# Layer 0's keys and values ahead of its queries, and a regrouped end, in a two-layer cross-attention and FFN kernel

## The chip, the cores and the metric

The kernel runs on one core of a Trainium2 chip. The time is the device time of one execution in microseconds (us), the median of several runs. PE is TensorE (PEld its weight loads), DVE is VectorE, ACT is ScalarE, POOL is GpSimd and SP is SyncE, which only issues DMAs. ACT issues some DMAs too.

## The reference, cut to what matters

The input is `x`, 8 tiles of 128 tokens by 512 values, and a context of the same shape. Four blocks follow each other, each added to `x` and each fed by a layer norm of it:

```python
x = x + L0_xattn(layernorm(x), ctx)   # Q = xn @ Wq + bq; K = ctx @ Wk + bk; V = ctx @ Wv + bv; 32 heads on 8 kv heads
x = x + L0_ffn(layernorm(x))          # router, 4 of 16 experts and a shared one
x = x + L1_xattn(layernorm(x), ctx)   # 32 heads of 128 on 4 kv heads
x = x + L1_ffn(layernorm(x))

def L1_ffn(xf):
    h = relu(layernorm(xf @ gw1.T + gb1) * gamma + beta)   # 32 columns a token
    gates = h @ gw2.T + gb2                                # 8 experts
    top_v, top_i = top_k(gates, 2); top_g = softmax(top_v)
    allowed = counts_of_each_expert_over_all_tokens <= capacity
    tmp = (xf @ lora_A) * w_of_each_expert                 # 128 columns a token
    return xf @ weight.T + (tmp @ lora_B) / 16
```

The count over all tokens is the one place in the last block where every tile needs every other.

## The kernel before, in words

The 8 tiles are worked in two halves of 4. Each engine's program is a hand-written list of calls; engines meet only at semaphores, and each engine runs its list strictly in order. PSUM has 8 banks, handed to PE's groups by `banks.take(n, piece, free)`, which makes PE wait until the bank's last reader is done. Products that need near-fp32 accuracy split each factor into a high and a low part (`_hi` is written by ACT, `_lo` by DVE) and use three matmuls (`three`).

**A normalization** of a tile (group `g`, tile `k`) goes: `norm_stats` on DVE (L403, L404), one `norm_sqrt` on ACT for a group of four (L411), `norm_recip` on DVE (L416), `norm_scale` on DVE (L433) into one of a few row buffers, `norm_turn` on PE (four 128x128 transposes, L442), `norm_hi` on ACT (L450 in groups 0 and 1, L453 elsewhere) and, from group 2 on, `norm_lo` on DVE (L460). Group 7 is the second half's rows for the last block. `mm_group` (L466) is the matmul line of nearly all products.

**The opening of layer 0.** `sync_attention0` issues the first loads on SP's queue in the order of the code. PE transposes `consts` 32 times (`WARM`, L698), turns the 4 normalized tiles of half 0 and computes queries 0 and 1 of half 0, the keys, queries 2 and 3, and the values of 4 tiles. A query (`query(half, m)`) and the keys are products of 512 columns in plain fp32, written out by ACT (`q0T_hi`, L758; `k0T_hi`, L750) and DVE (`q0T_lo`, L877; `k0T_lo`, L865), then sent by ACT's queue to DRAM (`q_rows`, L500; `k_rows`, L495). SP reads them back in another layout (`q0st`, L553 and L555; `k0bd`, L537 and L539). ACT splits the output weights (`wo_hi`, L763) in between. Next PE turns half 1's tiles, computes its keys and its query 0, and only then starts the scores (L645) of tile 0, which need all four queries of half 0 from DRAM. DVE has two jobs beside: the row maxima (`mx`, L886) of the scores and the normalization of half 1.

**The end.** Layer 1's attention runs 32 steps a half. In step `i` of the second half, `ending(i)` adds work of the last block: group 6's normalization, the adapter weights' split, and from `i == STEPS` the first half's small products. `tensor_small(h, 0)` is the gate product `h` of half `h` (32 columns), `tensor_small(h, 1)` the LoRA product `tmp` (128 columns) followed by the turn of `hT` (L2232). Then `tensor_adapters`: the dense products of tiles 0 to 3, with the turns of group 7 between them, both small products of half 1, the dense products of tiles 4 to 6 (`dense_open`, L2323, left open in their banks), the counts matmul (L2340), the dense product of tile 7, the turns of the expert weights `we` (L2347) and the LoRA products (L2358). DVE's gate work of half `h` is `vector_gating(h, 0..4)`: the norm of `h` (L2274 to L2289), the product with `gw2` (L2291 to L2294), the top two (L1298 to L2298), and the weights from the softmax (L2302 to L2306). ACT gives it a square root (j = 0, L2259) and an exponential (j = 3, L2262). `dense_add` (L2381) adds a dense product to `x`; L2413 adds the LoRA part, after which SP stores the tile.

```python
        def ending(i, weights, norm, norm_next, small):
            if STEPS - 4 <= i < STEPS:
                norm(6, i - STEPS + 7)
            if i == STEPS - 1:
                norm_next(7, 0)
            if i >= STEPS:
                small(0, i - STEPS)
```

Of the kernel before, what the change touches and what calls it, by code (L numbers as in the profile page):

```python
# [14 lines left out]
P = 128  # L15
# [109 lines left out]
def three(hi_lo_a, hi_lo_b):  # L125
    (ah, al), (bh, bl) = hi_lo_a, hi_lo_b
    return (ah, bh), (ah, bl), (al, bh)
# [38 lines left out]
def layers_kernel(nc, A, out):  # L166
    with ExitStack() as whole:
# [304 lines left out]
        WARM = 32  # L472
# [34 lines left out]
        def sync_attention0():  # L507
            load = nc.sync.dma_start
            load(consts[:, :], A["consts"]).then_inc(S["ld_consts"], 16)
            for b in range(HB):  # L510
                load(x[:, b, :], A["x"][b]).then_inc(S[f"rows_in{b}"], 16)
            load(wq[:, :, :], A["wq0"]).then_inc(S["ld_wq0"], 16)
            load(wkv[:, 0], A["wkv0"][:, 0]).then_inc(S["ld_wk0"], 16)
            load(ctxT[0][:, :, :], A["ctxT"][0]).then_inc(S["ld_ctx00"], 16)
            load(bq[:, :], A["bq0"]).then_inc(S["ld_bqk0"], 16)
            load(bk[:, :], A["bk0"]).then_inc(S["ld_bqk0"], 16)
            load(wkv[:, 1], A["wkv0"][:, 1]).then_inc(S["ld_wv0"], 16)
            load(bv[:, :], A["bv0"].broadcast_to([P, P])).then_inc(S["ld_wv0"], 16)
# [93 lines left out]
        def tensor_attention0():  # L612
# [133 lines left out]
        def scalar_attention0():  # L746
# [47 lines left out]
            norm_sqrt(0)  # L794
            for k in range(HB):
                norm_hi(0, k)
            query(0, 0)
            act.wait_ge(S["q0_lo"], 1)
            queries_out(nc.scalar, 0, 0)
            query(0, 1)  # L800
            act.wait_ge(S["q0_lo"], 2)
            queries_out(nc.scalar, 0, 1)
            keys(0)
            act.wait_ge(S["k0_lo"], 1)
            keys_out(nc.scalar, 0)
            norm_sqrt(1)
# [55 lines left out]
        def vector_attention0():  # L862
# [52 lines left out]
            query(0, 0)  # L915
            dve.wait_ge(S["ld_x_rest"], 16 * HB)
            norm_stats(1, 0)
            norm_stats(1, 1)
            query(0, 1)
            norm_stats(1, 2)  # L920
            keys(0)
            norm_stats(1, 3)
            query(0, 2)
            norm_recip(1)
            norm_scale(1, 0)
            query(0, 3)
            for k in range(1, HB):
                norm_scale(1, k)
            for b in range(HB):
                values(b)  # L930
# [1279 lines left out]
        def scalar_ending(i):  # L2210
            ending(i, scalar_adapter_weights, scalar_norm, scalar_norm, scalar_small)

        def vector_ending(i):
            ending(i, vector_adapter_weights, vector_norm, vector_norm, vector_small)

        def tensor_small(h, j):
            if j == 0:
# [7 lines left out]
            ps = banks.take(next(out_banks), ("tmp", h), (S["tmpT"], h + 1))  # L2225
            mm_group(ps[:, :], [q for k in range(KT) for q in three(
                (ws[0][:, k, 0:P], ws[1][:, k, 0:P]),
                (xn1[h][0][:, k, :], xn1[h][1][:, k, :]))]).then_inc(S["tmp_mm"], 1)
            ps = banks.take(next(out_banks), ("h_t", h), (S["gate_sc"], h + 3))
            pe.wait_ge(S["scT"], h + 3)  # L2230
            for b in range(HB):
                ins = nc.tensor.transpose(ps[:, b * G1:(b + 1) * G1], hT[h][:, b * P:(b + 1) * P],  # L2232
                                          ident[0:G1, 0:G1])
            ins.then_inc(S["gate_t"], 1)
# [83 lines left out]
        def tensor_adapters():  # L2318
# [6 lines left out]
            for b in range(HB):  # L2325
# [16 lines left out]
            dense_open(B - 1)  # L2342
            for h in range(2):
# [5 lines left out]
                ins.then_inc(S["we_t"], 1)  # L2349
            for b in range(B):  # L2350
# [10 lines left out]
        def scalar_adapters():  # L2361
            for b in range(HB):
                scalar_norm(7, b + 1)
            for j in (5, 6):
                scalar_norm(7, j)
            for j in (0, 3):
                scalar_gating(0, j)
            for j in range(2):
                scalar_small(1, j)
            for j in (0, 3):  # L2370
                scalar_gating(1, j)
# [4 lines left out]
        def vector_adapters():  # L2376
            for b in range(HB):
                vector_norm(7, b + 1)
# [3 lines left out]
            for j in (5, 6):  # L2382
                vector_norm(7, j)
            for j in range(5):
                vector_gating(0, j)
            for j in range(2):
                vector_small(1, j)
            for j in range(5):
                vector_gating(1, j)
# [152 lines left out]
```

## Time and profile before

| | before |
|---|---|
| median of 3 runs | 1236.09 us |
| lowest and highest run | 1232.84 and 1236.33 us |
| the profiled execution's time | 1236.35 us |
| its span, first to last instruction | 1235.0 us |
| PE busy | 1185.1 us, 96% |
| DVE busy | 805.3 us, 65% |
| ACT busy | 671.4 us, 54% |
| POOL busy | 419.6 us, 34% |
| mean granted TensorE clock | 0.992 |

The profiled execution takes 1.35 us more than its span. The chain that ended last is 82% PE, 7% DVE, 5% DMA and 3% ACT. A full clock (1.00) is TensorE's 2.4 GHz level, 0.50 its 1.2 GHz level. The change touches the first 50 us and the last 65.

### The profile page before, as it was taken

Reading aid. Unit: us, or ns where it says so; the run is one execution under the profiler, and the core shown is the slowest. Engines: PE = TensorE matmul, PEld = TensorE weight load, DVE = VectorE, ACT = ScalarE, POOL = GpSimd, SP = SyncE. Lnnn points to the kernel's source line nnn. Section 1 sums busy time; section 2 is a strip of 40 time slices with the busy share of each in tenths; the row PEclk is TensorE's granted clock in tenths of the full one; section 3 lists DMA queues with packets and bytes.
Section 4 is the critical chain, followed back from the end, with each engine's and each line's share of the span. In section 5 each row is a group of like instructions: output and inputs, shape, how many; then the busy total and the mean of one; then the engine's idle time right before and its main releaser. Section 6 shows DMA issues by size and latency. Waiting matters only on the chain.

```text
span 1235.0 us, 16580 instructions
## 1 busy us (share of the span) xinstructions
PE 1185.1 (96%) x5948; PEld 913.7 (74%) x5948; DVE 805.3 (65%) x1511; ACT 671.4 (54%) x1562; POOL 419.6 (34%) x515
## 2 busy tenths in 40 slices
PE   8989999899999999799999999999999999999997
PEld 5646556577776777688888888877888888888765
DVE  3457777677766784756666567764566666677757
ACT  2245741577777883355555555643455555556621
POOL 2413434577777761022223232310122232322200
PEclk9999999999999999899999999999999999999999
DMA  8675422885788777221112122211221121221101
GB/s 290 173 172 133 155 77 102 300 205 103 153 212 248 155 143 190 71 57 60 60 44 68 43 62 67 61 52 53 70 63 46 44 68 60 61 68 27 59 1 68
DMA packets 72849, 127.93 MB, mean 104 GB/s; under 512 B 11640, under 2 KB 30968, under 8 KB 70072
## 3 DMA queue, kind: packets, MB, share of 16 engines
q1 hardware_dynamic: 53024, 73.90, 20.1%
q0 software_dynamic: 17296, 48.26, 15.7%
q10 hardware_dynamic: 2448, 4.72, 1.1%
q8 instruction: 47, 0.77, 0.3%
q14 instruction: 34, 0.28, 0.1%
HBM read 150.37 MB, written 26.48 MB: 143 GB/s over the span
## 4 chain that ended last, share of the span: by engine, by line
PE 82%; DVE 7%; DMA 5%; ACT 3%; issue 2%; SPq 0%; ACTq 0%; POOL 0%; POOLq 0%; DVEq 0%
PE bank L466 50%; PE bank L1220 11%; PE bank L2008 7%; PE bank L1984 4%; PE bank L679 2%; PE bank L693 2%; PE bank L1280 2%; PE bank L645 1%; PE bank L660 1%; PE bank L1241 1%; DMA wf_raw<-in_wffn,weight_row 1%; DMA q0st<-m0T 1%; DMA lb_raw<-in_lb 1%; DMA returned<-moe 1%; DMA q_rows<-q0T_lo 1%
## 5 line engine op out<-in xcount | busy, mean ns | idle before, releaser
L1976 POOL TENSOR_SCALAR p<-p,mx 128x256 f32<-128x256 f32 x256 | 162.8, 652 | 524.4 <-DVE mx L1970 524.4
L1187 DVE TENSOR_TENSOR wf_lo<-wf_raw,wf_hi 128x512 fp32r<-128x512 f32 x188 | 121.5, 688 | 33.8 <-ACT wf_hi L1181 29.1
L1962 ACT ACTIVATE p<-bank,mx 128x256 f32<-128x256 f32 x256 | 118.0, 485 | 10.7 <-DVE mx L1952 10.5
L466 PE MATMUL bank<-xnA_hi,w1q_hi 128*128 128x512 f32 x288 | 118.6, 412 | 3.6 <-DVE xnA_lo L460 3.2
L1181 ACT ACTIVATE wf_hi<-wf_raw 128x512 fp32r<-128x512 f32 x192 | 110.1, 625 | 9.4 <-DMA wf_raw<-in_wffn,weight_row 9.0
L466 PE MATMUL bank<-xnA_hi,w1q_lo 128*128 128x512 f32 x288 | 114.6, 398 | 0.0
L466 PE MATMUL bank<-xnA_lo,w1q_hi 128*128 128x512 f32 x288 | 114.1, 396 | 0.0
L1991 ACT ACTIVATE p1T_hi<-bank 128x512 fp32r<-128x512 f32 x128 | 75.1, 596 | 65.7 <-PE bank L1984 65.7
L1916 ACT ACTIVATE q1T_hi<-bank 128x512 fp32r<-128x512 f32 x64 | 38.2, 597 | 132.2 <-PE bank L466 132.2
L466 PE MATMUL bank<-w1o_hi,a1T_hi 128*128 128x512 f32 x256 | 105.2, 411 | 0.1
L466 PE MATMUL bank<-wf_raw,zT 128*128 128x512 f32 x220 | 102.9, 593 | 2.2 <-DVE x L1263 1.3
L1922 DVE TENSOR_TENSOR q1T_lo<-bank,q1T_hi 128x512 fp32r<-128x512 f32 x64 | 44.2, 691 | 93.0 <-ACT q1T_hi L1916 93.0
L466 PE MATMUL bank<-w1o_hi,a1T_lo 128*128 128x512 f32 x256 | 100.3, 392 | 0.0
L466 PE MATMUL bank<-w1o_lo,a1T_hi 128*128 128x512 f32 x256 | 100.2, 391 | 0.0
L1603 POOL DMA_INDIRECT moe<-ys,token_out x47 | 82.1, 1746 | 28.1 <-issue 12.5
L2041 DVE TENSOR_TENSOR x<-bank,x 128x512 f32<-128x512 f32 x64 | 44.2, 690 | 71.8 <-PE bank L466 71.6
L1996 DVE TENSOR_TENSOR p1T_lo<-bank,p1T_hi 128x512 fp32r<-128x512 f32 x128 | 86.2, 681 | 0.0
L1948 DVE TENSOR_REDUCE mx<-bank 128x2 f32<-128x512 f32 x128 | 81.5, 677 | 0.0
L1220 PE MATMUL bank<-wf_hi,xsT_hi 128*128 128x512 f32 x188 | 78.4, 417 | 1.1 <-DVE xsT_lo L1293 1.1
L1984 PE MATMUL bank<-consts,p 128*128 128x128 f32 x512 | 75.5, 273 | 2.1 <-DVE a1T_lo L2019 2.1
L1220 PE MATMUL bank<-wf_lo,xsT_hi 128*128 128x512 f32 x188 | 74.1, 394 | 0.0
L1582 POOL DMA_INDIRECT wf_raw<-in_wffn,weight_row x47 | 50.5, 1075 | 66.9 <-PE bank L466 29.1
(338 smaller groups left out, 2958.8 us busy)
## 6 DMA issues: line engine op xcount, KB each, us to landing
w_raw<-in_wq SPq DMA_DIRECT2D x64, 256.0 KB
w_raw<-in_wo SPq DMA_DIRECT2D x64, 256.0 KB
moe<-xn SPq DMA_DIRECT2D x2, 2304.0 KB, 11.7
returned<-moe SPq DMA_DIRECT2D x8, 512.0 KB, 7.8
q0st<-q_rows SPq DMA_DIRECT2D x14, 256.0 KB, 4.6
x<-in_x SPq DMA_DIRECT2D x8, 256.0 KB, 6.5
ctx<-in_ctxT SPq DMA_DIRECT2D x2, 1024.0 KB, 10.8
q_rows<-q0T_hi ACTq DMA_DIRECT2D x8, 256.0 KB
```

What stands on the lines that cost most here:

```text
L466: ins = nc.tensor.matmul(ps, a, b, start=(n == 0), stop=(n == len(pairs) - 1))
L1181: nc.scalar.activation(wf[m % 2][0][:, a, c, :], raw[m % STREAMS][:, a, c, :], ACT.Copy).then_inc(S["gu_hi"], 1)
L1187: nc.vector.tensor_tensor(wf[m % 2][1][:, a, c, :], raw[m % STREAMS][:, a, c, :], wf[m % 2][0][:, a, c, :].bitcast(F32), ALU.subtract).the ...
L1220: ins = nc.tensor.matmul(ps[:, :], a, c, start=(k == 0 and t == 0), stop=(k == KT - 1 and t == 2))
L1603: nc.gpsimd.indirect_dma_start(out=moe[j % 2], out_offset=bass.IndirectOffsetOnAxis(ap=token_out[:, at:at + 1], axis=0), in_=ys[j % Y_RING ...
L1948: ins = nc.vector.tensor_reduce(m[:, 2 * n:2 * n + 2], banks.of(("s1", s, n))[:, :].rearrange("p (h k) -> p h k", h=2), AX.X, ALU.max)
L1962: ins = nc.scalar.activation(pr1[s % 2][:, h, :], banks.of(("s1", s, n))[:, hh * 2 * P:(hh + 1) * 2 * P], ACT.Exp, bias=m[:, UH + h:UH + h ...
L1976: ins = nc.gpsimd.tensor_scalar(pr1[s % 2][:, h, :], pr1[s % 2][:, h, :], m[:, 3 * UH + h:3 * UH + h + 1], 1.0, ALU.mult, ALU.mult)
L1984: ins = nc.tensor.transpose(ps[:, h * P:(h + 1) * P], pr1[s % 2][:, h, part * P:(part + 1) * P], ident)
L1991: nc.scalar.activation(p1T[0][:, part, :], banks.of(("t1", s, part))[:, :], ACT.Copy).then_inc(S["p1T_hi"], 1)
L1996: nc.vector.tensor_tensor(p1T[1][:, part, :], banks.of(("t1", s, part))[:, :], p1T[0][:, part, :].bitcast(F32), ALU.subtract).then_inc(S[" ...
L2008: ins = nc.tensor.matmul(ps[:, :], a, c, start=(part == 0 and n == 0), stop=(part == 1 and n == 2))
```

## The change

In the opening, the loads are issued in another order: the key weights and the context ahead of `x`, the query weights last. PE computes keys and values of half 0 ahead of the queries, with the turns between the values, and `WARM` is 20. ACT and DVE follow. At the end, DVE takes the statistics of group 7 tile by tile in steps STEPS-1 to STEPS+1, ACT the square root of group 7 in step STEPS+1, with a first square root of a constant in step STEPS-1. PE takes the gate product of half 1 between the dense products of tiles 1 and 2, and its turn ahead of the LoRA product. DVE's gate work of both halves is interleaved with the dense additions. The dense product of tile 7 goes behind the turns of `we`. No arithmetic is added but ACT's square root of one column.

```diff
-        WARM = 32
+        WARM = 20
...
             load(consts[:, :], A["consts"]).then_inc(S["ld_consts"], 16)
+            load(wkv[:, 0], A["wkv0"][:, 0]).then_inc(S["ld_wk0"], 16)
+            load(ctxT[0][:, :, :], A["ctxT"][0]).then_inc(S["ld_ctx00"], 16)
             for b in range(HB):
                 load(x[:, b, :], A["x"][b]).then_inc(S[f"rows_in{b}"], 16)
+            load(wkv[:, 1], A["wkv0"][:, 1]).then_inc(S["ld_wv0"], 16)
+            load(bk[:, :], A["bk0"]).then_inc(S["ld_bqk0"], 16)
+            load(bq[:, :], A["bq0"]).then_inc(S["ld_bqk0"], 16)
+            load(bv[:, :], A["bv0"].broadcast_to([P, P])).then_inc(S["ld_wv0"], 16)
             load(wq[:, :, :], A["wq0"]).then_inc(S["ld_wq0"], 16)
...
-            for k in range(HB):
+            keys(0, 7)
+            values(0, 4)
+            values(1, 5)
+            for k in range(2):
                 norm_turn(0, k, k)
-            query(0, 0, 4)
-            query(0, 1, 5)
-            keys(0, 7)
-            query(0, 2, 0)
-            query(0, 3, 1)
-            for b, n in enumerate((2, 3, 4, 5)):
-                values(b, n)
+            values(2, 6)
+            for k in range(2, HB):
+                norm_turn(0, k, k)
+            values(3, 4)
+            for m, n in enumerate((5, 6, 0, 1)):
+                query(0, m, n)
...
         def scalar_ending(i):
-            ending(i, scalar_adapter_weights, scalar_norm, scalar_norm, scalar_small)
+            if i == STEPS - 1:
+                nc.scalar.activation(hr[:, 0:1], eps, ACT.Sqrt)
+            if i == STEPS + 1:
+                norm_sqrt(7)
+            ending(i, scalar_adapter_weights, scalar_norm, nothing, scalar_small)
 
         def vector_ending(i):
-            ending(i, vector_adapter_weights, vector_norm, vector_norm, vector_small)
+            ending(i, vector_adapter_weights, vector_norm, vector_norm, nothing)
+            for k in (2, 3):
+                if i == STEPS + k - 2:
+                    dve.wait_ge(*norm_x_ready(7, k))
+                    norm_stats(7, k)
...
-            for b in range(HB):
-                if b >= 2:
-                    norm_turn(7, b - 2, next(out_banks))
...
-            for k in range(2, HB):
-                norm_turn(7, k, next(out_banks))
-            for j in range(2):
-                tensor_small(1, j)
-            for b in range(HB, B - 1):
+            for b in range(2):
+                for k in (2 * b, 2 * b + 1):
+                    norm_turn(7, k, next(turn_banks))
+                dense(b)
+            tensor_small(1, 0)
+            dense(2)
+            tensor_small(1, 2)
+            tensor_small(1, 1)
+            dense(3)
+            for b in range(HB, B - 2):
                 dense_open(b)
...
-            dense_open(B - 1)
+            dense_open(B - 2)
...
+            dense_open(B - 1)
             for b in range(B):
...
         def scalar_adapters():
...
+            norm_hi(7, 0)
+            norm_hi(7, 1)
+            scalar_gating(0, 0)
+            norm_hi(7, 2)
+            norm_hi(7, 3)
+            scalar_small(1, 0)
+            scalar_gating(1, 0)
+            scalar_gating(0, 3)
+            scalar_small(1, 1)
+            scalar_gating(1, 3)
...
         def vector_adapters():
...
+            norm_recip(7)
+            norm_scale(7, 0)
+            norm_scale(7, 1)
+            vector_small(0, 1)
+            norm_scale(7, 2)
+            norm_lo(7, 0)
+            norm_lo(7, 1)
+            norm_scale(7, 3)
+            vector_gating(0, 0)
+            vector_gating(0, 1)
+            norm_lo(7, 2)
+            norm_lo(7, 3)
+            dense_add(0)
+            vector_gating(0, 2)
+            vector_gating(0, 3)
+            dense_add(1)
+            vector_small(1, 1)
+            vector_gating(1, 0)
+            dense_add(2)
+            vector_gating(1, 1)
+            vector_gating(0, 4)
+            vector_gating(1, 2)
+            vector_gating(1, 3)
+            dense_add(3)
+            vector_gating(1, 4)
```

In the opening DVE's list becomes: scales of tiles 0 and 1 each followed by a tile's values, scales of tiles 2 and 3, keys, values 2 and 3, query 0, statistics of half 1's first two tiles, query 1, the other two, query 2, reciprocal and scale of half 1's tile 0, query 3, the other scales. ACT's is: square root, keys high, `norm_hi` four times, keys out, then each query high and out, with half 1's square root behind query 1 and two `wo_hi` behind queries 2 and 3 each, as before.

Three places show the order that results. First SP's queue in the opening, before and after; `wkv` is loaded twice, the keys' part first:

```order
L509 DMA consts<-in_consts 128x149
L511 DMA x<-in_x 128x512 x4
L512 DMA wq_66<-in_wq 128x2048
L513 DMA wkv_68<-in_wkv 128x512
L514 DMA ctx_0_64<-in_ctxT 128x2048
L515 DMA bq_86<-in_bq 128x4
L516 DMA bk_87<-in_bk 128x1
L517 DMA wkv_68<-in_wkv 128x512
L518 DMA bv_88<-in_bv 128x128
```

```order
L509 DMA consts<-in_consts 128x149
L510 DMA wkv_68<-in_wkv 128x512
L511 DMA ctx_0_64<-in_ctxT 128x2048
L513 DMA x<-in_x 128x512 x4
L514 DMA wkv_68<-in_wkv 128x512
L515 DMA bk_87<-in_bk 128x1
L516 DMA bq_86<-in_bq 128x4
L517 DMA bv_88<-in_bv 128x128
L518 DMA wq_66<-in_wq 128x2048
```

The query weights went from second to last, the keys' weights and the context to the front. Second, PE in the opening; `xn_58`, `xn_59`, `num` and `den` are the four normalized tiles, and the 128x128 products are values:

```order
-L698 MATMUL bank<-consts 128x128 x32
+L698 MATMUL bank<-consts 128x128 x20
+L466 MATMUL bank<-ctx_0_64,wkv_68 128x512 x4
+L466 MATMUL bank<-wkv_68,ctx_0_64 128x128 x8
 L442 MATMUL bank<-consts,xn_58 128x128 x4
 L442 MATMUL bank<-consts,xn_59 128x128 x4
+L466 MATMUL bank<-wkv_68,ctx_0_64 128x128 x4
 L442 MATMUL bank<-consts,num 128x128 x4
 L442 MATMUL bank<-consts,den 128x128 x4
```

Keys and two tiles of values now stand ahead of the turns; the values no longer stand between the last query and the turns of half 1. Third, ACT from step STEPS-1 on, before and after; `xnA` is half 0's normalized input, `xnB` half 1's:

```order
L2015 ACTIVATE a1T_hi<-bank 128x512
L453 ACTIVATE xnA_hi<-bank 128x4x128
L1991 ACTIVATE p1T_hi<-bank 128x512 x2
L2015 ACTIVATE a1T_hi<-bank 128x512
L2240 ACTIVATE hT_242<-bank,gb_240 32x512
L2244 ACTIVATE tmpT_259<-bank 128x512
L411 ACT_TABLE_LOAD
L411 ACTIVATE rstd<-moments,consts 128x4
```

```order
L2015 ACTIVATE a1T_hi<-bank 128x512
L2212 ACT_TABLE_LOAD
L2212 ACTIVATE hr<-consts 128x1
L453 ACTIVATE xnA_hi<-bank 128x4x128
L1991 ACTIVATE p1T_hi<-bank 128x512 x2
L2015 ACTIVATE a1T_hi<-bank 128x512
L2250 ACTIVATE hT_242<-bank,gb_240 32x512
L411 ACTIVATE rstd<-moments,consts 128x4
L2254 ACTIVATE tmpT_259<-bank 128x512
```

The table load and one short square root moved ahead of the last tile of `xnA_hi` and the last `p1T_hi`, and group 7's square root ahead of `tmpT`.

## Rows read from the trace of the kernel before

**Rows 1.** Chain of waits, opening: start us, length us, what worked or was waited for
```profile
2.59 5.21 DMA x<-in_x
...
12.72 14.02 PE bank L466 x32
...
32.69 6.71 DMA q_rows<-q0T_lo
```
**Rows 2.** Timeline, opening: start, length, engine, line, operation, count, [idle before <- releaser]
```profile
30.00 3.73 PE L466 MATMUL bank<-wkv,ctx 128*128 128x128 f32 x32
...
31.28 0.75 DVE L877 SCALAR_TENSOR_TENSOR q0T_lo<-bank,bq,q0T_hi 128x512 fp32r<-128x512 f32 x1 [2.38 <-ACT q0T_hi L758]
...
42.81 0.94 PE L645 MATMUL bank<-k0bd,q0st 96*128 96x256 f32 x6 [0.23 <-DMA q0st<-q_rows]
```
**Rows 3.** Timeline, SP's issues in the opening: start, length of the issue
```profile
4.01 0.43 SPq L514 DMA_DIRECT2D ctx<-in_ctxT  x1
...
6.59 0.68 SPq L518 DMA_DIRECT2D bv<-in_bv  x1
```
**Rows 4.** DMA issues, opening: KB each, us from issue to landing
```profile
ctx<-in_ctxT SPq DMA_DIRECT2D x1, 1024.0 KB, 10.2
bv<-in_bv SPq DMA_DIRECT2D x1, 64.0 KB, 10.4
```
**Rows 5.** DMA queues, 26 to 27 us (q10 is ACT's): packets, MB, share
```profile
q10 hardware_dynamic: 106, 0.20, 52.8%
```
**Rows 6.** Stretches: PE, PEld, DVE, ACT, POOL busy us (count), PEclk, DMA share, GB/s
```profile
42.80:47.30 4.50, 3.13 (x15) 2.12 (x16) 3.97 (x7) 0.51 (x1) 3.99 (x4) 1.00 0.96 212
47.30:50.70 3.40, 3.40 (x17) 3.40 (x18) 1.85 (x4) 0.00 (x0) 0.00 (x0) 0.51 0.71 190
...
1201.10:1204.20 3.10, 3.10 (x9) 1.28 (x8) 2.56 (x12) 1.58 (x2) 0.00 (x0) 0.50 0.02 5
```
**Rows 7.** Chain of waits, end
```profile
1191.16 2.80 PE bank L466 x12
1193.96 0.44 PE bank L442 x4
...
1199.81 0.69 DVE xnB_lo L460
...
1209.60 0.30 DVE h__244 L2251
...
1218.87 0.38 DVE chosen L2390
```
**Rows 8.** Timeline, end
```profile
1173.63 1.25 DVE L1996 TENSOR_TENSOR p1T_lo<-bank,p1T_hi 128x512 fp32r<-128x512 f32 x2
...
1174.81 0.39 PE L2008 MATMUL bank<-p1T_hi,v_hi 128*128 128x512 f32 x1
...
1181.87 0.69 DVE L2041 TENSOR_TENSOR x<-bank,x 128x512 f32<-128x512 f32 x1 [4.18 <-PE bank L466]
...
1219.38 0.37 PE L2340 MATMUL bank<-chosen,ones 128*128 128x16 f32 x2 [1.49 <-DVE chosen L2390]
...
1222.43 1.03 PE L2347 MATMUL bank<-consts,we 128*128 128x128 f32 x8
...
1227.05 1.28 DVE L2413 TENSOR_TENSOR x<-bank,x 128x512 f32<-128x512 f32 x2
```
**Rows 9.** Groups of DVE, 1184 to 1235 us: busy us, mean ns | idle before
```profile
L460 DVE TENSOR_TENSOR xnB_lo<-bank,xnB_hi 128x512 fp32r<-128x512 f32 x4 | 2.8, 692 | 0.8 <-ACT xnB_hi L453 0.8
L2381 DVE TENSOR_TENSOR x<-bank,x 128x512 f32<-128x512 f32 x4 | 2.8, 691 | 5.5 <-PE bank L466 5.5
...
L433 DVE TENSOR_SCALAR xn<-x,moments,rstd 128x512 f32<-128x512 f32 x4 | 2.2, 538 | 0.0
```
**Rows 10.** Timeline, a table load and what follows it on ACT at 51 us
```profile
51.47 1.28 ACT L827 ACT_TABLE_LOAD   x1
...
52.76 0.20 ACT L827 ACTIVATE preload<-consts 128x1 f32<-128x1 f32 x1
```

More of the change, by code:

```diff
@@ L794, in scalar_attention0 @@
             norm_sqrt(0)
+            keys(0)
             for k in range(HB):
                 norm_hi(0, k)
[L797 to L803, printed above, removed]
             act.wait_ge(S["k0_lo"], 1)
             keys_out(nc.scalar, 0)
+            for m in range(2):
+                query(0, m)
+                act.wait_ge(S["q0_lo"], m + 1)
+                queries_out(nc.scalar, 0, m)
             norm_sqrt(1)
@@ L914, in vector_attention0 @@
                 norm_scale(0, k)
-            query(0, 0)
-            dve.wait_ge(S["ld_x_rest"], 16 * HB)
[L917 to L926, printed above, removed]
+                if k < 2:
+                    values(k)
+            keys(0)
+            values(2)
+            values(3)
+            dve.wait_ge(S["ld_x_rest"], 16 * HB)
+            for m in range(KT):
+                query(0, m)
+                if m < 2:
+                    norm_stats(1, 2 * m)
+                    norm_stats(1, 2 * m + 1)
+                if m == 2:
+                    norm_recip(1)
+                    norm_scale(1, 0)
             for k in range(1, HB):
                 norm_scale(1, k)
-            for b in range(HB):
-                values(b)
             keys(1)
@@ L2224, in tensor_small @@
                 return
[L2225 to L2234, printed above, removed]
+            if j == 1:
+                ps = banks.take(next(out_banks), ("tmp", h), (S["tmpT"], h + 1))
+                mm_group(ps[:, :], [q for k in range(KT) for q in three(
+                    (ws[0][:, k, 0:P], ws[1][:, k, 0:P]),
+                    (xn1[h][0][:, k, :], xn1[h][1][:, k, :]))]).then_inc(S["tmp_mm"], 1)
+            if j == 2 or h == 0:
+                ps = banks.take(next(out_banks), ("h_t", h), (S["gate_sc"], h + 3))
+                pe.wait_ge(S["scT"], h + 3)
+                for b in range(HB):
+                    ins = nc.tensor.transpose(ps[:, b * G1:(b + 1) * G1], hT[h][:, b * P:(b + 1) * P],
+                                              ident[0:G1, 0:G1])
+                ins.then_inc(S["gate_t"], 1)
         def scalar_small(h, j):
@@ L2323, in dense_open, with dense @@
                     nc.tensor.matmul(ps[:, :], a, c, start=(n == 0), stop=False)
-            for b in range(HB):
-                if b >= 2:
-                    norm_turn(7, b - 2, next(out_banks))
+            def dense(b):
                 ps = banks.take(next(score_banks), ("dense", b), (S["dense_add"], b + 1))
@@ L2361, in scalar_adapters @@
         def scalar_adapters():
[L2362 to L2371, printed above, removed]
+            name, value = norm_dest_free[7]
+            act.wait_ge(S[name], value)
+            norm_hi(7, 0)
[8 more added lines that the diff above has]
+            scalar_gating(1, 3)
             for h in range(2):
@@ L2376, in vector_adapters, with dense_add @@
         def vector_adapters():
-            for b in range(HB):
-                vector_norm(7, b + 1)
+            def dense_add(b):
                 dve.wait_ge(S["dense_mm"], b + 1)
```

14 lines of the change are left out of this document (removed).

## The prediction, made before the changed kernel ran

> **What bounds the kernel now.** Read the chain of waits first, for who sets the end, then the timeline of the same stretch, for how long each piece takes and what idles. The page says PE is 96% busy and 82% of the chain, so a gain needs a stretch where PE idles or works beside the chain. There are two.
>
> In the opening the chain waits for `x` to land until 7.80, runs the normalization, and from 12.72 PE works without a gap: queries 0 and 1, keys, queries 2 and 3 [rows 1]. These five products end at 30.00, 17.28 / 5 = 3.46 us each; the values follow with 3.6 [rows 2]. Then come turns, keys and query 0 of half 1 until 42.58, and the scores begin at 42.81 after 0.23 us of waiting for a load [rows 2]. That load closes a round trip: the last query's low part is ready at 32.03 [rows 2], its store lands at 39.40 [rows 1], and SP reads it back. So PE and the round trip arrive within 0.23 us of each other.
>
> At the end the chain leaves PE at 1199.81 for DVE and stays there until `chosen` at 1219.24 [rows 7]: the gate work of half 0, then of half 1, one behind the other. PE waits 1.49 us for it before the counts at 1219.38 [rows 8], and its clock is at the 0.50 level (1.2 GHz) from 1201.10 to 1204.20 [rows 6]. The counts are followed by 15.6 us to the end of the span.
>
> **The end, worked out.** The same DVE work must fit between group 7's reciprocal and the counts, but interleaved, so I add up.
>
> First a cost. ACT gets a table load and a short square root, 1.28 + 0.20 = 1.5 us [rows 10], ahead of the last `xnA_hi` and the last `p1T_hi`. Queued behind them on ACT are these; for them waits DVE (`xnA_lo`, two tiles' statistics, `p1T_lo`), and for that PE's last attention product. Now the first `p1T_lo` ends near 1174.26 and PE takes it at 1174.81 [rows 8]: 0.55 us of slack, so PE starts 1.5 - 0.55 = 1.0 us late. Bounds: 0 if the load hides, 1.5 if the slack is gone.
>
> After the switch, the trace shows the next operation at 52.76, 0.01 us behind the load's end [rows 10]. The Trainium skill (ScalarE: Activation LUTs, "What ACT_TABLE_LOAD costs") counts a drain of about 1.38 us beside the load, 2.66 in all; by that the wait would be 2.4 instead of 1.0 and the time 1.4 higher. The trace does not agree at this place, so I leave it out of the sum and keep it as a rival.
>
> DVE: its last addition of layer 1 starts at 1181.87 now [rows 8], 1182.9 then. Addition 0.69, statistics 0.87, square root and reciprocal 0.5: scales begin about 1185.0. From there: 4 scales 2.2, 4 low parts 2.8, 4 dense additions 2.8 [rows 9], two copies 0.6 (0.30 each), `chosen` 0.4 [rows 7]. A half's gate work is 1219.24 - 1209.60 = 9.64 with copy and `chosen` [rows 7], so 8.9 without; some 0.3 us a half of that is waiting for ACT, which the interleaved additions now cover. Two halves 17.3. Sum 26.1: `chosen` ends at about 1211.1.
>
> PE: its last output product ends about 1182.7. Up to the counts it has the LoRA product of half 0, four dense products, both small products of half 1 and two open dense products, 9 x 2.80 = 25.2, and four turns of `xn` and two of `hT`, 6 x 0.44 = 2.6 [rows 7]: 1210.5, and 0.4 of waiting for DVE's last low part before the gate product. So 1210.9. The two meet within 0.2 us; the counts run at about 1211.2 instead of 1219.38, **8.2 us earlier**. PE no longer idles long enough there for the fall of rows 6 to return.
>
> Behind the counts nothing shortens: one dense product, then the turns of `we` 3.05 us after the counts, first final addition 4.62 us after those turns' start [rows 8]. The other dense product (2.80) now stands between the turns and the LoRA product, where PE was idle: turns end 1215.3, dense 1218.1, first LoRA product 1218.8, against 1218.9 for DVE's first addition. It is hidden with 0.1 to spare; uncovered it costs at most 2.8. Bounds of the gain: 9.2 (no delay from the table load) and 5.4 (that product uncovered).
>
> **The opening, worked out.** What matters is T, the start of the first query on PE: 12.72 now.
>
> Landings: `x` with 1.1 MB ahead and included lands at 7.80 [rows 1], the context with 3.4 MB at 4.01 + 10.2 = 14.2 and `bv` with 3.7 MB at 6.59 + 10.4 = 17.0 [rows 3, 4]. The first two give 2.8 us per MB. In the new order the context (1.4 MB) lands at 8.6, `x` (2.4) at 11.4, `bv` (2.7) at 12.3, or at 14.3 if it keeps its lag of 2.0 behind that line; the query weights, last with 3.7 MB, between 15.0 and 17.0. I take 14 for `bv`, since the same tiny loads stand ahead of it.
>
> The keys run from 8.6 to 12.1 in front. PE then waits for `bv`, which `values` demands together with its weights. Queued behind that wait are the turns; behind `values` on DVE stands the scale of tile 1. From `bv`, PE does four values (3.6) and four turns (1.8) before the first query: T = 19.4 at `bv` 14.0, 17.7 at 12.3. I take 19. Shorter warm-up: PE idles before the keys. The clock fell at 47.3 after PE had been busy 3.13 of 4.50 us [rows 6], so it may fall here; keys at the 1.2 GHz level would take 6.9 us, until 15.5, and add about 1.5 to T at most. Dropping 12 warm-up transposes costs nothing else, since PE would wait for the context anyway.
>
> From T: four queries end at T + 13.8. Before, the values (3.6) covered the latency from the last query to half 1's normalized tiles; now the turns are next. The last query's low part ends 2.0 us behind the product (30.00 to 32.03 [rows 2]), the scales of tiles 1 to 3 follow at 0.54 each, the last turn 0.44: T + 17.9 instead of T + 15.6. A new wait of 2.3. Keys and query of half 1, 7.0: scores at T + 24.9. With T = 19 that is 43.9, against 42.81: **1.1 us later**. Break-even is T = 17.9.
>
> The round trip: 12.8 us from the last query's end to the scores would give T + 26.6 = 45.6, 2.8 later. But ACT's queue now carries five pairs of stores back to back at 0.20 MB/us [rows 5], 0.52 MB a pair, 2.6 us each; with the queries 3.46 apart and the keys' pair out of the way, the last pair has no queue ahead. I count 2 us less or more, T + 24.6, and keep 2.8 as the bound. The other bound is T = 17, a gain of 0.9.
>
> SP's queue is moved past nothing else; the number of DMAs is unchanged. POOL waits for the normalized tiles and for `wo_hi`, both later by some 4 us, beside PE's work. Everything between 50 and 1170 us I let slide with the scores: 0.
>
> **Sum.** 1235.0 - 8.2 + 1.1 = 1227.9 of span, and 1.35 around it as in the profiled execution (1236.35 against a median of 1236.09): 1229.2. The shown runs spread over 3.5 us, so I add 1.5 on both sides.
>
> **Rivals.**
> 1. *Forecast*: 1229.2. For it: both sums at the end agree. Chance 0.54.
> 2. *The opening gains.* `bv` lands on the line and the queries start at 17: -0.9 instead of +1.1, and the table load hides: 1226.2. For it: the lag of `bv` may come from what was issued with it, not from the tiny loads ahead. Chance 0.16.
> 3. *The opening pays double.* The round trip sets the scores (+2.8), or the clock falls once there and costs 1.7 (half of the 3.4 us at the lower level [rows 6]): +2.8 to +4.5, 1231 to 1232.6. Chance 0.14.
> 4. *A new wait in the end takes the cover.* DVE and PE are within 0.2 us in three places; if the dense product of tile 7 or an ACT operation queued behind another holds the chain, the gain is 5.4 instead of 8.2: 1232.0; with the delays of both, up to 1234. Chance 0.10.
> 5. *The drain of the table switch is paid*: 1230.6 by the working above. Against it: rows 10. Chance 0.03.
> 6. *Slower than before.* SP's queue serves the loads it holds together rather than in turn; then the query weights, now last of the urgent ones, land with the 3.3 MB queued behind them, 9.2 us later, T about 26.2. Opening +8.3: 1236.4, no change; with the clock at its lower level for two stretches more, 1240. It decides from T = 26.1 on, and means slower by 0.3% only from T = 29.8. Against it: `x` landed 6.4 us ahead of the context. No change 0.02, slower 0.01.
>
> That the change doesn't do what it says: the order shows that it does.
>
> **How the numbers follow.** A measurement can tell about 0.3%, 3.7 us, from no change. Faster means below 1232.4. Rival 4 and the worst of rival 3 reach over it: half of 4 and a quarter of 3, with the rest of 6, make 0.11 for no change, 0.01 for slower, 0.88 for faster. The range goes from 1224.7 (rival 2 less 1.5) to 1233.5 (rival 4's 1232.0 and 1.5 more; it holds rival 3 and 5 as well).
>
> **What would show it.** First query on PE at 19 (17.7 to 20), scores at 43.9; PE idle between the last query of half 0 and the turns of half 1. At the end: a table load at about 1171 in the old time, PE waiting about 1 us before its last attention product, no stretch at 0.50 after 1180, the counts about 28.5 us after the last output product's end instead of 37.7, and 15.6 us from counts to end. Wrong would be: counts less than 6 us earlier relative to the last output product, a first query past 22, or a difference of over 2 us grown between 50 and 1170 us.

## The result, and the profile after

The kernel before took 1235.8 us (median of 13 runs, 1232.84 to 1238.54), the changed one 1228.97 us (13 runs, 1225.48 to 1232.93). The ratio is 0.9948, with a 95% interval of 0.9935 to 0.996: 6.4 us less, between 4.9 and 8.0. The forecast was 1229.2, with a range of 1224.7 to 1233.5. The profiled execution took 1227.31 us, its span is 1226.0 (before 1236.35 and 1235.0).

The end first. The chain of waits of the changed kernel, start and length in us:

```profile
1170.36 1.28 ACT L2212
...
1174.68 0.58 DVE p1T_lo L1996
...
1175.31 1.67 PE bank L2008 x6
...
1205.15 5.48 PE bank L2333 x24
1210.64 0.13 PE bank L2354 x2
1210.76 2.83 PE bank L2333 x12
1213.59 0.45 PE bank L2361 x4
...
```

The long run of DVE in [rows 7] is gone: the chain now goes over PE's dense product (L2333), the counts (L2354), the dense product of tile 6, and the turns of `we` (L2361). A shorter run of DVE stays in the chain, from 1186.86 to 1193.14, but PE is busy beside nearly all of it. The timeline of the same stretch:

```profile
1171.66 0.20 ACT L2212 ACTIVATE hr<-consts 128x1 f32<-128x1 f32 x1
...
1175.31 0.50 PE L2008 MATMUL bank<-p1T_hi,v_hi 128*128 128x512 f32 x1 [0.76 <-DVE p1T_lo L1996]
...
1182.53 0.69 DVE L2041 TENSOR_TENSOR x<-bank,x 128x512 f32<-128x512 f32 x1 [3.37 <-PE bank L466]
...
1209.87 0.37 DVE L2424 TENSOR_REDUCE chosen<-goh 128x16 f32<-128x128 f32 x1
...
1210.47 0.29 PE L2354 MATMUL bank<-chosen,ones 128*128 128x16 f32 x2
...
1213.43 1.03 PE L2361 MATMUL bank<-consts,we 128*128 128x128 f32 x8
...
1218.06 1.28 DVE L2447 TENSOR_TENSOR x<-bank,x 128x512 f32<-128x512 f32 x2
```

PE waits 0.76 us for the last `p1T_lo`, because the table load and its square root stand ahead of it on ACT. Layer 1's last addition starts at 1182.53, against 1181.87 in [rows 8]. The counts start at 1210.47 without a wait: 27.9 us after that addition, where it was 37.5 (1219.38 less 1181.87). `chosen` ends at 1210.24, 0.2 us ahead of them. From the counts to the end of the span it is 15.5 us, as before. By stretches (us, then PE, PEld, DVE, ACT and POOL busy with counts, granted clock, DMA share, GB/s):

```profile
1183.00:1193.30 10.30, 10.09 (x55) 7.97 (x54) 8.89 (x30) 3.37 (x7) 0.00 (x0) 1.00 0.00 0
1193.30:1210.60 17.30, 17.30 (x78) 12.92 (x79) 15.25 (x66) 3.21 (x6) 0.00 (x0) 1.00 0.01 1
```

PE is busy for all but 0.2 us of 27.6, and the clock stays at 1.00; the 3.1 us at 0.50 of [rows 6] don't return.

Now the opening, timeline of PE:

```profile
2.65 4.20 PE L698 MATMUL bank<-consts 128*128 128x128 f32 x20 [2.65 <-DMA consts<-in_consts]
7.46 3.67 PE L466 MATMUL bank<-ctx,wkv 128*128 128x512 f32 x8 [0.62 <-DMA ctx<-in_ctxT]
12.77 2.05 PE L466 MATMUL bank<-wkv,ctx 128*128 128x128 f32 x16 [1.64 <-DMA bv<-in_bv]
...
18.25 13.97 PE L466 MATMUL bank<-xnF,wq 128*128 128x512 f32 x32
32.06 0.60 PE L442 MATMUL bank<-consts,xn 128*128 128x128 f32 x4
35.13 0.66 PE L442 MATMUL bank<-consts,xn 128*128 128x128 f32 x4 [2.47 <-DVE xn L433]
...
36.60 3.60 PE L466 MATMUL bank<-ctx,wkv 128*128 128x512 f32 x8
...
44.49 0.94 PE L645 MATMUL bank<-k0bd,q0st 96*128 96x256 f32 x6 [0.86 <-DMA q0st<-q_rows]
```

and the round trip of the last query in the chain of waits:

```profile
31.59 1.15 ACT wo_hi L765 x2
32.74 0.58 ACT q0T_hi L760
33.35 0.76 DVE q0T_lo L877
34.13 0.59 ACTq L500
34.76 6.48 DMA q_rows<-q0T_lo
```

The context lands about 1.2 us ahead of the forecast, `bv` 1.3 us, and the first query starts at 18.25 instead of 19. The wait ahead of half 1's turns is there (2.47). PE would be ready for the scores at about 43.6, and then waits 0.86 us for a load that closes the round trip of the last query: its product ends at 32.06 and the scores start at 44.49, 12.4 us later. They are 1.7 us later than in [rows 2]. The store takes 6.48 us, nearly as long as before (6.71, [rows 1]), and a queue stands ahead of it. The ten stores of half 0's keys and queries are 1360 packets on q10, ACT's queue, so 136 each. When the first store of the last pair was issued, the queue had moved this much, first in the kernel before (0 to 32.06 us), then in the changed one (0 to 34.13 us):

```profile
q10 hardware_dynamic: 879, 1.70, 13.7%
```

```profile
q10 hardware_dynamic: 953, 1.85, 16.2%
```

The four older pairs are 1088 packets, so 209 of them were still to go before and 135, one whole store, in the changed kernel. The queue ahead got shorter by half a store and did not vanish.

### The profile page after: what moved, and what is told of

The parts are those of the page before. It is cut to its first block, busy times and chain, and to the rows that moved or that the text cites. A ratio compares the mean times of both kernels' runs of the same rounds, so it can differ in the third digit from the quotient of the medians.

```text
span 1226.0 us, 16554 instructions
## 1 busy us (share of the span) xinstructions
PE 1180.0 (96%) x5936; PEld 911.9 (74%) x5936; DVE 804.8 (66%) x1511; ACT 669.7 (55%) x1561; POOL 419.6 (34%) x515
## 4 chain that ended last, share of the span: by engine, by line
PE 70%; POOL 7%; DVE 7%; issue 7%; DMA 5%; ACT 3%; SPq 1%; ACTq 0%; POOLq 0%; DVEq 0%
PE bank L466 46%; PE bank L2008 7%; PE bank L1220 5%; PE bank L1984 4%; POOL moe L1603 4%; POOL xs L1592 2%; PE bank L679 2%; PE bank L693 2%; DMA moe<-ys,token_out 1%; PE bank L645 1%; POOL wf_raw L1582 1%; PE bank L660 1%; DMA xs<-xn_rows,token_in 1%; PE bank L2333 1%; DMA q0st<-m0T 1%
## 5 line engine op out<-in xcount | busy, mean ns | idle before, releaser
L1948 DVE TENSOR_REDUCE mx<-bank 128x2 f32<-128x512 f32 x128 | 81.5, 677 | 0.0
```

The costliest lines, as they stand in the source:

```text
L1948: ins = nc.vector.tensor_reduce(m[:, 2 * n:2 * n + 2], banks.of(("s1", s, n))[:, :].rearrange("p (h k) -> p h k", h=2), AX.X, ALU.max)
```

## The experiments

Each ratio is against the kernel before, run on the same chip beside it. Where places are compared, they come from one profiled execution each. From the scores' start to the last row maximum of layer 1's attention (L1948) the executions of the thirteen kernels differ by up to 4.6 us (1114.0 to 1118.6), with the same code there; so a whole span tells little, and the places are compared by distances inside a stretch.

### The end alone, and the opening alone

`e1_end_only` has the changed functions of the end and the opening of the kernel before; `e2_open_only` the reverse.

> The opening as before, the end as changed. Theory A (the end gives all of it, the opening costs what its scores are late, 1.7 us at 44 us): the scores start at 42.8 and the whole is 1 to 2 us below the changed kernel, near 1227.5. Theory B (a late opening is taken up by later waits before layer 1): scores at 42.8, but the whole within 0.7 us of the changed kernel, near 1229. From the last output product of layer 1 to the end of the span both expect 43.5 us, as in the changed kernel, against 53 before.

> The opening as changed, the end as before. Theory A: scores at 44.5 and 1 to 2 us slower than before, 1237 to 1238. Theory B: scores at 44.5, but the same time as before within 0.7 us; the lateness of 1.7 us at 44 us should then be found smaller at each later landmark (138, 185, 227 us).

The end alone: 1225.72 us, ratio 0.993 (0.9916 to 0.9944), so 8.6 us less (6.9 to 10.4). The opening alone: 1236.36 us, ratio 1.0015 (1.0004 to 1.0027), so 1.9 us more (0.5 to 3.3). Together they give -6.7, the whole change measured -6.4. Both fit theory A, the end alone with a little more than the 1 to 2 us forecast. In the opening alone the scores start at 45.02, in the end alone at 42.39; from layer 1's last addition to the end it is 43.5 us with the new end and 53.2 with the old one. The old opening has its scores at 42.4 to 43.0 in its three profiled kernels, so one execution tells such a place to about half a microsecond. So the whole gain is made at the end, and the opening gives some of it back.

In the opening alone it was not the round trip that held the scores. Timeline and stretch of `e2_open_only`:

```profile
36.85 5.30 PE L466 MATMUL bank<-ctx,wkv 128*128 128x512 f32 x8
41.98 3.60 PE L466 MATMUL bank<-xnF,wq 128*128 128x512 f32 x8
45.02 1.15 PE L645 MATMUL bank<-k0bd,q0st 96*128 96x256 f32 x5
```

```profile
37.00:40.00 3.00, 3.00 (x5) 1.18 (x4) 0.00 (x0) 1.76 (x4) 3.00 (x5) 0.50 0.75 225
```

The keys of half 1 take 5.3 us instead of 3.6 at a granted clock of 0.50 (1.2 GHz), right behind the 2.47 us in which PE waited for the normalized tile. Of the seven profiled kernels that have this order of PE (the changed one, and e2, e3, e5, e6, e7, e11), five show the low clock there; of the six that have the values behind the last query (before, and e1, e4, e8, e9, e10) none does. Where PE at its low clock sets the scores, they start 12.6 to 12.7 us after the last query's end; where the round trip does (the changed kernel, e3), 12.4 to 12.5. The two nearly coincide. (`e6` is left out here: another wait holds its scores.) Why the clock fell in five and not in the changed kernel and e3, which have the same wait, stays open.

### Values back behind the last query

The load order, the keys in front and the changed end stay. DVE's list follows; its part of the edit is left out here.

```
-            values(0, 4)
-            values(1, 5)
-            for k in range(2):
-                norm_turn(0, k, k)
-            values(2, 6)
-            for k in range(2, HB):
+            for k in range(HB):
                 norm_turn(0, k, k)
-            values(3, 4)
-            for m, n in enumerate((5, 6, 0, 1)):
+            for m, n in enumerate((4, 5, 0, 1)):
                 query(0, m, n)
+            for b, n in enumerate((2, 3, 6, 4)):
+                values(b, n)
```

> The changed kernel with the values moved back behind the last query of half 0, keys and load order as changed. Theory A: the first query no longer waits for bv but for the query weights at about 16.0, against 18.25; the values cover the wait in front of half 1's turns again (2.5 us of idle PE in the changed kernel, under 0.3 here), so the scores start at 42.2 (both by PE's work and by the round trip of 12.4 us from the last query), 2.3 us earlier than changed. The whole gains 1 to 2 us if A, under 0.7 if B. Rival: the query weights land later once nothing waits between, first query at 18, scores at 44.

1226.34 us, ratio 0.9932 (0.9918 to 0.9946). Timeline of PE:

```profile
15.48 13.97 PE L466 MATMUL bank<-xnF,wq 128*128 128x512 f32 x32 [1.16 <-DMA wq<-in_wq]
29.29 3.73 PE L466 MATMUL bank<-wkv,ctx 128*128 128x128 f32 x32
32.86 1.27 PE L442 MATMUL bank<-consts,xn 128*128 128x128 f32 x8
...
42.78 0.95 PE L645 MATMUL bank<-k0bd,q0st 96*128 96x256 f32 x6 [0.91 <-DMA q0st<-q_rows]
```

The queries no longer wait behind `bv`, and the values again cover the latency to half 1's turns. The scores are back at 42.8. With 13.5 us from the last query's end to the scores it is the round trip that holds them; PE is ready 0.9 us earlier. I had counted on 12.4 us and 42.2. The last pair found 231 older packets ahead of it in ACT's queue (857 of 1088 moved by 31.36), against 135 in the changed kernel, so queries that end 2.8 us earlier gave only 1.7. The order of the values is what the opening loses by, not the order of the loads: the trace shows it, and the medians agree (2.0 us), though the intervals of the two ratios overlap.

### The table load one step later

```
-            if i == STEPS - 1:
+            if i == STEPS:
                 nc.scalar.activation(hr[:, 0:1], eps, ACT.Sqrt)
```

> The changed kernel with ACT's constant square root, and so its table load, one step later (behind the last a1T_hi instead of ahead of the last xnA_hi). Theory A: PE's wait of 0.76 us before its last attention product goes, all that follows moves up by 0.8 us relative to the last step, and the table load still hides, since ACT idles there for over 2 us. Rival: the load then delays hT of half 0 and with it the LoRA bank, and nothing is gained. In the whole 0.8 us is near the limit of what the comparison tells; the trace decides.

1228.17 us, ratio 0.9944 (0.9929 to 0.9958). Timeline:

```profile
1174.74 0.39 PE L2008 MATMUL bank<-p1T_hi,v_hi 128*128 128x512 f32 x1
...
1176.92 1.28 ACT L2212 ACT_TABLE_LOAD   x1
```

PE's wait is gone. From the last row maximum of layer 1 (L1948) to the last output addition it takes 21.2 us here and 22.3 in the changed kernel; the kernel before has 21.2. All profiled kernels with the load at its early place have 22.3 or 22.4, all with it later or without it 21.2 or 21.3. So the load costs 1.1 us where the change put it and nothing one step later. In the medians this is too small to be seen (0.9944 against 0.9948).

### The dense product of tile 7 back ahead of the turns

```
             dense_open(B - 2)
+            dense_open(B - 1)
             for h in range(2):
...
-            dense_open(B - 1)
             for b in range(B):
```

> The changed kernel with the dense product of tile 7 back ahead of the turns of we; nothing else differs. The prediction's working: between turns and the first LoRA product PE has nothing but this product, so with it ahead the turns start one dense product (2.8 us) later, at 1216.4 on the changed kernel's clock, and the last six additions follow: end of span 2.3 to 2.8 us later, from the last output addition to the end 46 instead of 43.5, 1231 to 1232. Rival (DVE or ACT, still at work on we, holds the turns anyway, so that the product was hidden in either place): less than 0.5 us.

1230.86 us, ratio 0.9971 (0.9956 to 0.9987), 2.8 us more than the changed kernel's ratio gives, though the intervals touch; the trace decides. Chain of waits, and the timeline of PE behind the turns:

```profile
1213.07 0.14 PE bank L2354 x2
1213.21 5.58 PE bank L2333 x24
1218.79 0.45 PE bank L2362 x4
```

```profile
1218.63 1.03 PE L2362 MATMUL bank<-consts,we 128*128 128x128 f32 x8
1221.45 0.47 PE L2373 MATMUL bank<-lb_hi,la_hi 128*128 128x512 f32 x1 [1.78 <-issue]
```

Now 5.58 us of dense products stand between counts and turns instead of 2.83, and PE idles 1.78 us behind the turns. From the last output addition to the end it is 46.3 us against 43.5. The product costs its full 2.8 ahead of the turns and nothing behind them, where DVE and ACT work on `tw` and `la`.

### What makes the last store slow

SP reads nothing of the queries back before all four stores of half 0 have landed.

```
         for m in range(KT):
+            sp.wait_ge(S[f"st_q{m}"], 32)
+        for m in range(KT):
```

> The changed kernel, where SP starts no read of the queries' rows before all four stores of half 0 have landed. It tells what makes the last query's store land 6.5 us after it was issued. Theory A (SP's reads share the path with ACT's stores): the last store lands 3 to 4.5 us after its issue, and ACT's queue moves about 0.20 MB in each us of its flight; the scores may still be later, since four reads now follow one another. Theory B (stores of ACT's own queue, issued before, stand ahead of it): it lands 6 to 7 us after issue as before, with the queue still at 0.1 to 0.2 MB/us, and the scores are 2 to 4 us later.

One execution, 1234.43 us. Chain of waits:

```profile
36.61 4.62 DMA q_rows<-q0T_lo
...
50.23 1.78 DMA q0st<-q_rows
```

The last store lands 4.62 us after its issue, against 6.48. The queues (q1 is SP's, q10 ACT's; packets, MB, share), 34 to 35 us in the changed kernel:

```profile
q1 hardware_dynamic: 88, 0.04, 14.2%
q10 hardware_dynamic: 63, 0.12, 44.1%
```

and alone, 28 to 29 us and 34 to 35 us in this kernel:

```profile
q10 hardware_dynamic: 105, 0.20, 53.1%
```

```profile
q10 hardware_dynamic: 46, 0.09, 39.5%
```

The two microseconds of this kernel have no reads beside them, and one moves less than the changed kernel with reads. While the last store flies the queue moves 0.05 to 0.19 MB in each us, not the 0.20 of theory A, and the kernel before moved 0.20 to 0.21 from 28 to 30 us with SP's reads beside it. So the reads are not what sets the rate here. What theory B names is there too: when the last store was issued, 315 packets were left to move, itself included (1045 of 1360 moved by 36.61), in the changed kernel 369 (991 by 34.76), in the kernel before 427 (933 by 32.69). The times to landing go the same way: 4.62, 6.48 and 6.71 us. That is 68, 57 and 64 packets in a us. At the changed kernel's 57 the smaller queue alone would give 5.5 us, so about half of the 1.9 us is the queue ahead; the rest, at most 0.9 us, may be the reads or the spread of the rate, and one execution does not part them.

Holding the reads back is no way out: SP then issues them one behind the other, 0.43 us each, and the scores start at 52.15. I had expected 2 to 4 us for that; it was 7.7, of which 1.9 because its queries ended later. Of those 1.9 us, 0.2 are a later `bv` and 1.7 the clock: behind its wait of 1.95 us for `bv` the granted clock was 0.50 from 15 to 17 us, over the values and the turns, where the changed kernel has 1.00.

### The biases' load, the warm-up

`e11_bv_first` issues `bv` ahead of `x`; `e7_warm32` has 32 warm-up transposes again.

> The changed kernel with one load moved: bv goes out ahead of x instead of behind the value weights and the small biases. PE waits for bv 1.6 us ahead of the values in the changed kernel. If bv's own landing is what holds the first query: that wait goes or falls to about 0.3 (the value weights land next), the first query starts at 17 instead of 18.3, the scores at 43 instead of 44.5, ratio 0.994. If the value weights issued with it land as late, or x lands later because of the broadcast load ahead of it: first query at 18 to 19 and no change, 0.9948.

> The changed kernel with the old number of warm-up transposes, 32 instead of 20. The prediction's step: PE waits for the context and then for bv anyway, so the twelve cost nothing either way. Keys would start when the transposes end, about 2.5 us later than 7.5, at 9.3 to 10, or at the context's landing; the values would still start at bv, 12.8, and the first query at 18.3. Rival (keys then end after bv has landed): the first query 0.2 to 1 us later. The clock stays at its high level in both.

With `bv` first: 1227.54 us, ratio 0.9945 (0.9925 to 0.9964), no change. PE then waits for the value weights instead, 0.98 us, and the values start at 12.53 instead of 12.77. It was not `bv` alone that was late but what was issued with it. With the warm-up (one execution, 1230.68 us) the keys start at 7.62 instead of 7.46, the values at 12.94 and the first query at 18.42. The warm-up makes no difference that can be told here; my 9.3 to 10 for the keys was wrong, because the twelve added transposes take only 0.9 us (5.11 against 4.20). The clock stayed high up to the queries but fell at the keys of half 1, which I had not expected.

### Towards a better version

`e8_best` joins the values behind, the late table load and the changed end. `e9_end_late_table` is the opening of the kernel before with the changed end and the late table load. `e10_wq_first` is `e8_best` with the query weights loaded ahead of the value weights:

```
-            load(wkv[:, 1], A["wkv0"][:, 1]).then_inc(S["ld_wv0"], 16)
             load(bk[:, :], A["bk0"]).then_inc(S["ld_bqk0"], 16)
             load(bq[:, :], A["bq0"]).then_inc(S["ld_bqk0"], 16)
-            load(bv[:, :], A["bv0"].broadcast_to([P, P])).then_inc(S["ld_wv0"], 16)
             load(wq[:, :, :], A["wq0"]).then_inc(S["ld_wq0"], 16)
+            load(wkv[:, 1], A["wkv0"][:, 1]).then_inc(S["ld_wv0"], 16)
+            load(bv[:, :], A["bv0"].broadcast_to([P, P])).then_inc(S["ld_wv0"], 16)
```

> The changed kernel with two of its pieces corrected: the values of half 0 stand behind the last query again (the keys stay in front, the loads keep the new order), and the constant's square root that brings ACT's table stands one step later. Theory A (the two measured apart add up: values behind gave 2.6 us over the changed kernel, the later table 0.7): 1225 to 1226 beside a kernel before of 1235.8, ratio 0.992 to 0.993; first query on PE near 15.5, scores near 42.8, no wait of PE ahead of its last attention product, 43.5 us from layer 1's last output addition to the end. Theory B (the later table gives nothing, since the same wait of PE turns up at another operation): the ratio of the kernel with the values behind alone, 0.9932.

> The opening of the kernel before, the changed end, and the table's load one step later. If the new opening with the values behind is worth nothing over the old opening, this runs level with the combination of all three (within 0.1%), 1225 to 1226, ratio 0.992 to 0.993; if the keys in front still gain, it is slower than that by 0.5 to 1 us. Against the same kernel without the later table (ratio 0.993) it should gain 0.5 to 1.0 us; scores at 42.4, PE without a wait ahead of its last attention product.

> The kernel with values behind, late table and changed end, and now the query weights loaded right behind x, ahead of the value weights and bv, since the first query waited for them 1.2 to 1.7 us. Theory A (the scores follow the end of the last query by a round trip of 12.4 to 13.7 us, so what brings the first query forward brings the scores forward): first query at 15.0 to 15.3 instead of 16.0, scores at 41.8 to 42.2, about 0.7 us less than that kernel, ratio 0.992 to 0.993. Theory B (the loads share the path, so that the order of the last three changes nothing): first query at 15.5 to 16.0, ratio as before, 0.9935.

| kernel | median us | ratio (95%) | last query's product ends | scores start |
|---|---|---|---|---|
| changed | 1228.97 | 0.9948 (0.9935 to 0.996) | 32.06 | 44.5 |
| e8_best | 1225.42 | 0.9937 (0.9916 to 0.9958) | 29.83 | 42.7 |
| e9_end_late_table | 1226.1 | 0.9927 (0.9905 to 0.9949) | 29.2 | 43.0 |
| e10_wq_first | 1225.09 | 0.9912 (0.9896 to 0.9928) | 29.14 | 42.5 |

`e8_best`, `e9_end_late_table` and the two kernels e1 and e4 can't be told apart (0.9927 to 0.9937). So the later table load did not show in the medians beside e1 or e4, and keys in front with the values behind gained nothing over the old opening. The three kernels with the changed end that have the changed order of PE in the opening and tile 7's product where the change put it (the changed one, e3, e11) lie at 0.9944 to 0.9948. `e10_wq_first` has the lowest ratio of all, 10.9 us less than before (8.9 to 12.8), and its interval lies below the changed kernel's: by these five runs it beats both, though it was not run beside the changed kernel. Its interval overlaps those of `e8_best`, `e9_end_late_table`, e1 and e4. Its first query starts at 15.30 and waits only for the turned tiles, so the loads bound it no longer. But the scores gained 0.1 us against `e8_best`, not 0.7, since the round trip took 13.4 us instead of 12.9:

```profile
31.83 6.98 DMA q_rows<-q0T_lo
```

The places explain 0.1 us of the difference between these two; the rest of the 0.25% is inside the intervals and is not shown. The last query's product ends anywhere from 29.1 to 30.0 in the six kernels with the values behind, and SP's first read behind the last store is issued at 38.7 to 39.7 without a relation to it (29.14 and 38.83 in e10, 29.2 and 39.73 in e9, 29.83 and 38.86 in e8). In all six ACT's queue still holds older stores when the last pair comes (181 packets in e8, where it comes at 31.90, 209 in the kernel before at 32.06, 248 in e10 at 31.21, 280 in e1 at 31.13), so an earlier last query finds a longer queue ahead, and gains little.

## Why the prediction was right, step by step

The forecast time of 1229.2 us came within 0.3 us of the median. That is closer than the steps deserve: a difference of 7.1 us was forecast and 6.4 measured, the end gave 0.4 more than worked out and the opening cost 0.8 more, and the mechanism in the opening was not the one forecast.

**The end, -8.2 forecast.** The sum was right in mechanism and 0.4 us low: alone it measured -8.6, and from layer 1's last addition to the end 9.7 us went (53.2 to 43.5), where I had 9.2 before taking off the 1.0 of the table load. `chosen` took 27.7 us from that addition where the sum gave 28.2. PE's and DVE's ends meet within 0.2 us, as worked out, and neither waits for the other for long.

**The table load, 1.0.** Right: 1.1 us by the late placing. The operation behind the load starts 0.02 us after its end (1170.36 and 1.28, then 1171.66). Rival 5 with its drain of 1.38 us falls. The Trainium skill (ScalarE: Activation LUTs, "What ACT_TABLE_LOAD costs") counts that drain with every switch; my estimate from it was that PE would be 2.4 us late, and the measurement, 1.1, decides against it here.

**The dense product of tile 7, hidden.** Right: the final additions start 4.63 us after the turns with the product between them (1213.43 to 1218.06), 4.63 us without it in `e5_dense7_back` (1218.63 to 1223.26), and 4.62 in [rows 8]. Its uncovered price, 2.8, is what `e5_dense7_back` measured.

**The opening, +1.1 forecast.** Right in sign, too small: +1.7 to the scores in the profiled execution, +1.9 (0.5 to 3.3) in the medians. Two steps failed, and they partly cancel.

- T was 18.25, not 19, since `bv` landed 1.3 us earlier than the 14 I took. With `bv` at 14.0 my own sum gives 19.4, and 1.3 less is 18.1. The lag of `bv` behind the line of bytes was mostly not its own: it landed at 12.73, 0.4 behind the line where it had been 2.0. The 17 of rival 2 does not come out of that sum either, which gives 17.7 at the earliest.
- "The last pair has no queue ahead. I count 2 us less" was wrong. I had taken the queue at 0.20 MB/us, 2.6 us a pair, and the keys' pair out of the way. But the keys' first packets moved only after 21 us, when 3.5 us had passed since their issue, and the queue moved 0.11 to 0.20 MB in a us from 23 to 34; so it never ran empty, and the last pair found 135 older packets ahead of it. The trip became 0.4 us shorter (12.8 to 12.4), not 2. So the round trip, not PE, set the scores. It is the first mechanism of rival 3, which I priced at 2.8 with T at 19; with T at 18.25 and a trip of 12.4 us it gave 1.7. PE itself would have been ready at T + 25.4, where I had T + 24.9.

**The clock, 1.7 in rival 3.** I had named it for the shorter warm-up, ahead of the keys of half 0. There it did not fall. It fell behind the new wait that I had worked out myself, in five of seven profiled kernels, and in `e6_reads_wait` once more behind the wait for `bv`; I had not connected waits and clock there. On top of the round trip the fall at the keys of half 1 costs no more than 0.3 us, because the two end at nearly the same time.

**The middle, 0.** Not decided. In the two profiled executions the middle is 2.1 us shorter in the changed kernel (1117.8 to 1115.7 from the scores to the last row maximum), which is over the 2 us that I had named as a sign of being wrong. But the executions of all kernels differ there by 4.6 us without a relation to the opening, so the sign was set inside the noise. The span went down by 9.0 us in this pair: 9.7 at the end less 1.1 for the table load and 1.7 for the opening, and the 2.1 of the middle. In the medians, the sum of the two parts measured apart agrees with the whole within 0.3 us.

## What to carry to other kernels

When work is moved ahead of the operation that starts a long round trip through DRAM, the round trip moves with it, whatever is won beside it; what was there before as a cover for the next latency leaves a wait of its own. Whether a transfer has a queue ahead is read from what was issued and what had moved by its issue, not from one good rate. So ask of every product in an opening whether it feeds the longest trip or can lie under it, and load the weights in that order. An activation table load that is moved out of a waiting stretch is only free where ACT has a full gap: where the change put it, it cost 1.1 us here, and one step later nothing.

## What the runs showed of the hardware beside it

ACT's queue got nothing at first while SP's loads were in flight: the stores of the keys were issued at 17.51 and 18.70, yet in the changed kernel the microsecond from 20 to 21 shows SP's queue alone, and the next one the first packets of ACT's:

```profile
q1 hardware_dynamic: 120, 0.44, 106.7%
```

```profile
q1 hardware_dynamic: 54, 0.32, 77.2%
q10 hardware_dynamic: 29, 0.06, 15.2%
```

And ACT's stores alone don't go over 0.20 MB in a microsecond at half the engines' share, where SP's loads move 0.44; in some microseconds they move 0.05 to 0.10 with nothing beside them (`e6_reads_wait`, 0.09 from 34 to 35 us). Why the one queue had to wait, and what holds the stores at 0.20 and below, these runs don't tell.
